# Second attention layer: key blocks added on GpSimd, denominators of 256 columns, query scores one pair further ahead

## What is computed

```python
    def _L1_attn_ref(x, Wq, Wk, Wv, Wo):
        ...
        scores = jnp.einsum('bhqd,bhkd->bhqk', q, k) / scale
        causal = jnp.triu(jnp.ones((T, T), dtype=bool), k=1)
        scores = jnp.where(causal, jnp.asarray(-jnp.inf, scores.dtype), scores)
        attn = jax.nn.softmax(scores, axis=-1)
        ctx = jnp.einsum('bhqk,bhkd->bhqd', attn, v)
        out = ctx.transpose(0, 2, 1, 3).reshape(B, T, HEADS * D_V)
        return out @ Wo
```

## Time and profile before

| | |
|---|---|
| time, median of 3 runs | 949.31 us (949.01 to 952.53) |
| the profiled execution's own time | 950.26 us |
| its span, first to last instruction | 948.5 us |
| mean granted TensorE clock | 0.937 |
| TensorE busy (matmuls) | 790.8 us, 83% |
| VectorE busy | 575.1 us, 61% |
| ScalarE busy | 472.5 us, 50% |
| GpSimd busy | 296.2 us, 31% |

### The profile page before, as it was taken

How to read it: one execution, slowest core, us unless ns; L and a number is a source line. 1 busy time by engine, 2 the same in 40 slices (tenths; PEclk the granted TensorE clock), 3 DMA queues, 4 the chain that set the end, 5 groups by cost and what they waited for, 6 DMA issues and landing times. The chain is left out here.

```text
span 948.5 us, 19520 instructions
## 1 busy us (share of the span) xinstructions
PE 790.8 (83%) x7061; PEld 451.7 (48%) x7061; DVE 575.1 (61%) x1715; ACT 472.5 (50%) x750; POOL 296.2 (31%) x437
## 2 busy tenths in 40 slices
PE   1588989998829999179999999999999999739970
PEld 0234444444316778125555555555555555534430
DVE  4458999999531111244576776666666656324687
ACT  0377888887812222035454545445455444306664
POOL 3012333333336000424344444434443322100152
PEclk9989999999958999679999999999999999878995
DMA  0274333433215553221454444333334332210002
GB/s 26 72 239 124 97 89 96 108 84 89 69 32 129 158 149 88 67 59 45 96 96 96 96 96 92 74 86 78 81 76 96 79 85 51 56 45 0 1 0 89
DMA packets 111705, 78.02 MB, mean 82 GB/s; under 512 B 12272, under 2 KB 103088, under 8 KB 111616
## 3 DMA queue, kind: packets, MB, share of 16 engines
q1 hardware_dynamic: 107984, 71.16, 30.5%
q0 software_dynamic: 3344, 5.56, 2.2%
q10 hardware_dynamic: 288, 0.13, 0.1%
HBM read 37.86 MB, written 13.63 MB: 54 GB/s over the span
## 5 line engine op out<-in xcount | busy, mean ns | idle before, releaser
L1375 DVE TENSOR_REDUCE l_neg_max<-l_by_query 128x6 bf16<-128x768 f32 x128 | 122.5, 957 | 129.9 <-PE l_by_query L1121 129.6
L1447 POOL TENSOR_SCALAR_AFFINE_SELECT l_probs<-l_probs 128x512 f32<-128x512 f32 x128 | 87.1, 680 | 190.9 <-ACT l_probs L1250 190.7
L493 ACT ACTIVATE l_probs<-l_ps_s,minus_bound 128x1024 f32<-128x1024 f32 x128 | 137.9, 1116 | 2.3 <-PE l_ps_s L367 1.4
L1250 ACT ACTIVATE l_probs<-l_by_key 128x768 f32<-128x768 f32 x128 | 103.8, 811 | 68.1 <-PE l_by_key L1151 63.9
L1166 PE MATMUL l_ps_c<-l_probs,l_values 128*64 128x256 f32 (+1 forms) x1024 | 113.5, 343 | 0.0
L1166 PEld LDWEIGHTS l_ps_c<-l_probs,l_values 128*64 128x64 f32 x1024 | 62.9, 138 | 39.7 <-issue 21.2
L1190 PE MATMUL l_ps_v<-w_o,l_ctx 128*128 128x128 f32 x512 | 68.6, 290 | 15.1 <-DVE l_ctx L1393 15.1
L382 PE MATMUL l_ps_o<-l_probs,l_vpad 128*32 128x256 f32 x1024 | 80.6, 397 | 0.2
L1103 PE MATMUL l_ps_v<-w_v,l_xT 128*128 128x512 f32 x128 | 72.8, 651 | 0.4 <-ACT l_values L1271 0.2
L1190 PEld LDWEIGHTS l_ps_v<-w_o,l_ctx 128*128 128x128 f32 x512 | 62.6, 200 | 20.9 <-DVE l_ctx L1393 15.5
L1271 ACT ACTIVATE l_values<-l_ps_v 128x512 f32<-128x512 f32 x64 | 38.2, 597 | 65.4 <-PE l_ps_v L1103 60.0
(11 more groups left out here) (229 smaller groups left out, 1422.5 us busy)
## 6 DMA issues: line engine op xcount, KB each, us to landing
l_rrep<-rden_d SPq DMA_DIRECT2D x32, 512.0 KB
q_ring<-l_parts SPq DMA_DIRECT2D x192, 64.0 KB
k_ring<-l_parts SPq DMA_DIRECT2D x192, 64.0 KB
w<-in_L_ffn_w_dram SPq DMA_DIRECT2D x32, 256.0 KB, 3.0
disp_d<-zeros SPq DMA_DIRECT2D x8, 320.0 KB, 3.7
l_xin<-in_L_attn_x_dram SPq DMA_DIRECT2D x16, 128.0 KB, 3.1
l_xr<-in_L_attn_x_dram SPq DMA_DIRECT2D x16, 128.0 KB, 2.5
x_d<-l_x SPq DMA_DIRECT2D x16, 128.0 KB, 2.1
```

What stands on the lines that cost most here:

```text
L493: act.activation(probs[c % RING][:, :], ps_s[c % 2][:, :], ACT.Exp, bias=k["minus_bound"][:, :], scale=SCALE).then_inc(probs_sb, 1)
L1250: act.activation(probs[c % P_RING][:, :, 0:N + P], by_key[:, :, 0:N + P], ACT.Exp, scale=SCALE).then_inc(p_sb, 1)
L1375: dve.tensor_reduce(neg_max[:, :, half, :, h].rearrange("p a u -> p u a"), by_query[:, :, 0:3 * P].rearrange("p u (a q) -> p u a q", a=3), ...
L1447: pool.affine_select(out=corners, in_=corners, compare_op=ALU.is_ge, fill=0.0, base=0, pattern=[[0, 4], [1, P]], channel_multiplier=-1).th ...
```

## The change

Three edits. **One**: behind `context(b, c)`, GpSimd adds the columns of key block 1 onto the last 128 columns of key block 0, in place (`add_blocks`); the denominators then need four matmuls over 256 columns each instead of eight over 256 and 128, and wait for the additions (`both_sb`). For this `context` counts every pair in `ctx_ps`. **Two**: the ring `probs` has six buffers, counted over the batches, and the denominators run later behind their context; those of pairs 6 and 7 move into the next step. **Three**: `scores_by_query` and `maxima` run one pair further ahead, and the lists of all compute engines are written anew around this. SyncE's list is unchanged.

```diff
-P_RING = 4
+P_RING = 6
...
             def denominators(b, j):
                 if real(b):
                     if j == 0:
                         at_least(pe, rden_sb, b)
-                    for kb, first, q0 in ((0, 0, 0), (1, N, P)):
-                        for g in range(4):
-                            u, e = divmod(g, 2)
-                            last = pe.matmul(ps_d[32 * g:32 * g + 32, q0:N], sums[:, j, :],
-                                             probs[(2 * j + e) % P_RING][:, u, first:first + N - q0],
-                                             start=j == 0 and kb == 0, stop=j == QUADS - 1 and kb == 1)
+                    pe.wait_ge(both_sb, b * PRE + 2 * j + 2)
+                    for g in range(4):
+                        u, e = divmod(g, 2)
+                        last = pe.matmul(ps_d[32 * g:32 * g + 32, 0:N], sums[:, j, :],
+                                         probs[(b * PRE + 2 * j + e) % P_RING][:, u, 0:N],
+                                         start=j == 0, stop=j == QUADS - 1)
                     last.then_inc(sum_ps, 1)
...
             def step(b):
-                x_by_channel(b + 2)
                 scores_by_key(b, 2)
                 context(b, 0)
-                scores_by_query(b + 1, 1)
+                denominators(b - 1, 3)
+                x_by_channel(b + 2)
+                scores_by_query(b + 1, 2)
...
                 scores_by_key(b, 7)
                 context(b, 5)
-                denominators(b, 2)
                 values_of(b + 1, 3)
-                scores_by_query(b + 1, 6)
+                scores_by_query(b + 1, 7)
 
                 scores_by_key(b + 1, 0)
                 context(b, 6)
+                denominators(b, 2)
                 project(b - 1, 0)
-                scores_by_query(b + 1, 7)
+                scores_by_query(b + 2, 0)
 
                 scores_by_key(b + 1, 1)
                 context(b, 7)
-                denominators(b, 3)
                 project(b - 1, 1)
                 maxima_by_head(b + 1, 1)
-                scores_by_query(b + 2, 0)
+                scores_by_query(b + 2, 1)
...
             def step(b):
+                maxima(b + 1, 2)
                 reciprocals(b - 1)
+
                 add_attention(b - 2)
-                maxima(b + 1, 1)
+                maxima(b + 1, 3)
...
+                maxima(b + 1, 5)
 
                 second_input(b + 3)
-                maxima(b + 1, 4)
-
                 divide(b - 1, 0)
                 divide(b - 1, 1)
-                maxima(b + 1, 5)
+                maxima(b + 1, 6)
...
+            def add_blocks(b, c):
+                if real(b):
+                    pool.wait_ge(ctx_ps, b * PRE + c + 1)
+                    pr = probs[(b * PRE + c) % P_RING]
+                    pool.tensor_tensor(pr[:, :, P:N], pr[:, :, P:N], pr[:, :, N:N + P], ALU.add).then_inc(both_sb, 1)
```

More of the change, by code:

```diff
@@ L1168, in context @@
                                              pr[:, u, first:first + N - q0], start=kb == 0, stop=kb == 1)
-                    if c % 2:
-                        last.then_inc(ctx_ps, 1)
+                    last.then_inc(ctx_ps, 1)
             def denominators(b, j):
@@ L1195, in step @@
             def step(b):
[L1196 removed]
                 scores_by_key(b, 2)
                 context(b, 0)
[L1199 removed]
+                denominators(b - 1, 3)
+                x_by_channel(b + 2)
+                scores_by_query(b + 1, 2)
                 scores_by_key(b, 3)
                 context(b, 1)
[L1203 removed]
                 queries_keys(b + 2)
[L1205 removed]
+                scores_by_query(b + 1, 3)
                 scores_by_key(b, 4)
                 context(b, 2)
+                denominators(b, 0)
                 values_of(b + 1, 0)
[L1210 removed]
+                scores_by_query(b + 1, 4)
                 scores_by_key(b, 5)
                 context(b, 3)
[L1214 removed]
+                maxima_by_head(b + 1, 0)
                 values_of(b + 1, 1)
[L1216 removed]
+                scores_by_query(b + 1, 5)
                 scores_by_key(b, 6)
                 context(b, 4)
[L1220 removed]
+                denominators(b, 1)
                 values_of(b + 1, 2)
[L1222 removed]
+                scores_by_query(b + 1, 6)
                 scores_by_key(b, 7)
                 context(b, 5)
[L1226 removed]
                 values_of(b + 1, 3)
[L1228 removed]
+                scores_by_query(b + 1, 7)
                 scores_by_key(b + 1, 0)
                 context(b, 6)
+                denominators(b, 2)
                 project(b - 1, 0)
[L1233 removed]
+                scores_by_query(b + 2, 0)
                 scores_by_key(b + 1, 1)
                 context(b, 7)
[L1237 removed]
                 project(b - 1, 1)
                 maxima_by_head(b + 1, 1)
[L1240 removed]
+                scores_by_query(b + 2, 1)
             steps(step)
@@ L1274, in context_out @@
                 if real(b):
-                    act.wait_ge(ctx_ps, b * QUADS + j + 1)
+                    act.wait_ge(ctx_ps, b * PRE + 2 * j + 2)
                     at_least(act, wo_ps, b - 1)
@@ L1285, in step @@
             def step(b):
+                exponential(b, 2)
                 x_out(b + 2)
-                exponential(b, 2)
                 exponential(b, 3)
                 context_out(b, 0)
+                exponential(b, 4)
                 high_part(b + 2)
-                exponential(b, 4)
                 values_out(b + 1, 0)
@@ L1406, in step @@
             def step(b):
+                maxima(b + 1, 2)
                 reciprocals(b - 1)
                 add_attention(b - 2)
-                maxima(b + 1, 1)
+                maxima(b + 1, 3)
+                lower_parts(b + 2)
+                third_input(b - 2)
+                maxima(b + 1, 4)
                 add_expert(b + 3)
-                maxima(b + 1, 2)
-                third_input(b - 2)
-                lower_parts(b + 2)
-                maxima(b + 1, 3)
+                maxima(b + 1, 5)
                 second_input(b + 3)
-                maxima(b + 1, 4)
                 divide(b - 1, 0)
                 divide(b - 1, 1)
-                maxima(b + 1, 5)
+                maxima(b + 1, 6)
                 divide(b - 1, 2)
                 divide(b - 1, 3)
-                maxima(b + 1, 6)
                 maxima(b + 1, 7)
                 maxima(b + 2, 0)
+                maxima(b + 2, 1)
             steps(step)
@@ L1467, in step @@
                 mask(b, 2)
+                add_blocks(b, 0)
+                mask(b, 3)
+                add_blocks(b, 1)
                 root(pow3, x3_step, (b - 2) * X3 + 1 + 2 * NB, mv3, veps3, rstd3, b - 2)
-                mask(b, 3)
-                root(pow2, x2_step, (b + 3) * X2 + 3 * NB, mv2, veps2, rstd2, b + 3)
                 mask(b, 4)
+                add_blocks(b, 2)
                 low_part(b + 2)
                 mask(b, 5)
+                add_blocks(b, 3)
+                mask(b, 6)
+                root(pow2, x2_step, (b + 3) * X2 + 3 * NB, mv2, veps2, rstd2, b + 3)
+                add_blocks(b, 4)
+                mask(b, 7)
+                add_blocks(b, 5)
                 gather(b + 4)
-                mask(b, 6)
-                mask(b, 7)
                 mask(b + 1, 0)
+                add_blocks(b, 6)
                 mask(b + 1, 1)
+                add_blocks(b, 7)
             steps(step)
```

18 lines of the change are left out of this document (6 added, 12 removed).

## The result

| | before | after |
|---|---|---|
| median, us | 949.16 (943.57 to 952.53, 4 runs) | 990.05 (982.54 to 997.29, 4 runs) |
| profiled execution, us | 950.26 | 982.54 |
| its span, us | 948.5 | 980.8 |
| busy: TensorE, VectorE, GpSimd, % of the span | see the table of before | 80, 60, 40 |

The profiled execution is the fastest of the four, 32.3 us above the profiled one of before. I account for those 32.3 us; the other runs have 5 to 15 us more.

What follows compares the result with a forecast made beforehand. TensorE's work and a chain from VectorE's reduction through SyncE's list to the key scores were taken to bound each step. 950.26 + 34.3 (order and smaller terms) + 26 (clock) = 1010.6, less 0.95: 1009 us, range 978 to 1028.

Steps and rivals of the forecast that it cites:

- rival A: Later reciprocal delays SyncE's list as forecast, but the clock does not fall because work divides the pause: 984 us, chance 0.19.
- The chain: Reduction, reciprocal, SyncE's list, rows, key scores: starting later, it makes TensorE wait 3.6 us; +2.3 us a step, +30.2 us.
- The clock: TensorE's pauses drop its clock to half in most steps: 2.0 us in each of thirteen steps, +26 us.
- The fill: While the pipeline fills, the input of batch 1 is turned one pair later: +1.0 us.
- Step 14 and the end: Step 14 has no loads behind the reciprocal, -0.5 us; step 15 has later reciprocal and last denominators, +3.6 us.
- The denominators: On TensorE, a group without its second half takes 0.54 us instead of 0.78, saving 0.96 us a step.
- The additions: GpSimd's eight additions a step take 0.6 us each (0.58 to 1.16), and cost nothing as long as nobody waits.
- Rival B: VectorE's divisions become the last wait, slowed by contention with GpSimd: 1 us more a step, 1022 us, chance 0.09.
- Rival C: SyncE's list has hidden slack, so the later reciprocal moves nothing and TensorE bounds: 930 us, chance 0.07.

Runs made afterwards that it cites:

- all the mends together: Changed kernel with VectorE's reciprocal ahead of pair-2 maxima, second layer norm behind pair-7 maxima, SyncE's `xa` load before read-back, rows before last two loads: 940.59 us.
- no additions: Changed kernel without GpSimd's eight additions, so its denominators leave out key block 1: 1010.62 us, ratio 1.064.
- order alone: Changed kernel's order and ring of six, with the denominators of before in two forms and no additions: 1007.96 us, ratio 1.059.
- second input late: Changed kernel with VectorE's normalisation that waits for GpSimd's root moved behind the pair-7 maxima: 998.33 us, ratio 1.050.
- the first experiment: Changed kernel with VectorE's reciprocal moved ahead of the pair-2 maxima, nothing else: 961.03 us, ratio 1.011.

## Why the prediction was right, and where it was off

The verdict and the mechanism held: slower, 990 us inside 978 to 1028, and the later reciprocal with SyncE's list behind it is the cause. Undoing the one move on VectorE gave back 29 of 41 us, shortening the list alone gave 12, and all the mends together turned the loss into a gain. The size did not hold: 60 us of loss were forecast (the sum written down gives 1009.6) and 41 measured, and 990 lies inside the range because its lower end was set by rival A's price, not by the forecast's own terms. By its own steps, for the 32.3 us of the profiled execution, with the thirteen steps of the table:

- **The chain, +2.3 us a step.** Measured +1.6 in the nine steps without a fall (27.3 against 25.6 us). The list did start later: in the step shown, key scores to key scores across the chain is 19.54 us (20.1 forecast), the rest 7.77 (7.87). The chain was 16.9 us instead of 17.6, because write to key scores took 14.3 us against 14.95 in the step of before. TensorE's pause is 3.2 us (3.6 forecast). Some 21 us in all instead of 30.2.
- **The clock, +2.0 us in each of thirteen steps.** This is the step that failed. "So most steps should pay": four did, and they are 2.8 us longer, 11 us instead of 26. The price was about right: 1.8 us of the 2.8 are work at the low clock, the rest the longer pause. Their number was three times too high. I had seen two pieces of pause, and took 0.5 us of work as too little to part them; there are three, since VectorE is also late at pair 5. The Trainium skill (TensorE: Matmul & The Clock Gate, HAM oscillation) has the pattern of bursts and waits; the trace agrees with it in the four steps, and not in the other nine, where three pauses like the 1.1, 1.4 and 0.75 us of the step shown left the clock at 1.00. Where the pauses joined (no additions, order alone, second input late), 7 to 9 stretches fell and the time came to 998 to 1011 us, where my forecast lay. So the clock term was nearer right for other kernels than this.
- **The fill, +1.0.** +0.4, from the first query-key product of the layer to pair 2 of batch 1. The layer's start itself came 1.45 us earlier (392.29 against 393.74), in stages that the change does not touch.
- **Step 14 and the end, +3.1.** +0.8 measured: step 14 was 0.6 us shorter (0.5 forecast), the rest 1.4 longer instead of 3.6. Why the end cost less, no run shows.
- 32.5 us in the thirteen steps, -1.45, +0.4 and +0.8 make the 32.3.
- **The denominators, 0.54 us a group:** 0.57. **The additions, 0.6 us:** 0.73, 1.15 at most, inside the bounds of 0.58 and 1.16, and off the path but for one wait of 0.7 us.
- **Rival A** (the chain, no falls, 984 us) describes nine of the thirteen steps. It names the profiled time nearly, but by errors that cancel: its chain and its end were too large, and there were falls.
- **Rival B** (divisions and contention) was no cause of the loss, since without the additions it grew. The Trainium skill (SBUF — State Buffer, Who interferes with whom) says that such a VectorE instruction and a GpSimd one exclude each other; the trace agrees: a pair of divisions takes 1.28 us by itself, 1.74 beside a mask (before, where there are no additions) and 2.22 beside a mask and an addition. I had priced it as time on the path. Its effect was to spread the pauses in most steps; in two of the four steps with a fall such a longer pair, behind a late read-back, is part of the pause ahead of the fall.
- **Rival C** is excluded: the list had no slack. Moved ahead of two loads (1.3 us of issues), its rows gave 12 us.
- What I did not see at all is the second limit: GpSimd's root behind the mask of pair 6, then VectorE's normalisation, divisions and reduction. It is why the first experiment took back 29 and not 41 us, together with the row waits left (4.3 us).

Left open: why the read-back of the denominators lands later when the second input goes late (the divisions could start 11.0 us behind the write in the step I looked at, 10.4 in the full change without a wait for it; in that step SyncE issued the read-back 3.5 us behind the write instead of 1.7, which is as far as the trace leads), which pauses bring a fall and which do not, and how the runs of the change up to 15 us slower than the profiled one divide into falls and waits; only one was profiled.

## What to carry to other kernels

When a step is moved on one engine, look for the queue whose list begins with a wait for it: the list nearly kept its length here (16.9 and 17.6 us from reduction to key scores), so the delay came out at its end, one batch further. A wait of a few tenths of a microsecond in most steps marks a second limit, and behind it may stand a third; mend one alone and the next takes its place, so mend them together before judging the change. And taking work or a wait away can join the pauses that are left: the split ones cost only themselves in nine of thirteen steps here, while the kernels with joined pauses had seven to nine stretches at half the clock.

## What the runs showed of the hardware that I had not expected

- Less work was slower, and more work was free. Without the additions steps 1 to 13 took 17 us more (382.2 against 365.5); with two useless products a step they took no longer than without (379.2 and 381.3). Both go with the number of stretches at a granted clock near 0.5: 4 in the change, 8 without additions, 7 and 3 for the order without and with the filler.
- A step with a low stretch had 1.4 to 2.7 us more of TensorE busy time, 1.8 on average, inside what I had set (0 to 2.9).
- A pause need not be 3 us long for it: 2.70 us behind one of 0.64 did it, and 1.22 and 1.36 with 0.5 us of work between, while 0.92, 1.22 and 0.59 in one step did not. Nor did 1.22 and 1.29 at 554.17 and 556.12, nor a single 2.50 in the order alone.
- GpSimd's in-place addition of 256 columns takes 0.73 us, more than its mask of 512 columns (0.64), and 1.15 us when it meets a division on VectorE, which then is longer too (the pair 2.22 us, beside a mask and an addition; 1.28 alone).
